# A four-layer network in one kernel: the skip term of the second scan summed by TensorE, and another order of the first mixer chunk

## The chip, the cores and the metric

The kernel runs on one core of a Trainium2 chip. Its time is the device time of one execution in microseconds (us); the median over several executions is compared. The engines run side by side and wait for each other through semaphores: TensorE (PE), VectorE (DVE), ScalarE (ACT), GpSimd (POOL), and the queue of SyncE (SP), from which all DMAs are issued.

## What is computed

2048 tokens of 128 numbers pass four layers, each added to its input. Cut to what matters here:

```python
x = L0_attn_u                                                  # 1 x 2048 x 128
x = x + _L0_attn_ref(_layernorm(x), ...)   # "mixer": projection, causal conv, state-space scan of 8 heads, gate
x = x + _L0_ffn_ref(_layernorm(x), ...)    # causal attention of 16 heads, then 8 experts, 2 per token
x = x + _L1_attn_ref(_layernorm(x), ...)   # "scan": the layer below
x = x + _L1_ffn_ref(_layernorm(x), ...)    # "net": a gated net of 512 hidden values

# of the mixer, for each token t and head:
h = exp(dt_t * A) * h + dt_t * x_t * B_t ;  y_t = C_t . h + D * x_t
# of the scan layer, for each of 256 channels and 16 states:
h = exp(-delta * n) * h + delta * B_n * u
y = h.sum(-1)
y = y + u * D          # the skip term, D is one number per channel
y = y * silu(z)
return y @ out_proj_w + out_proj_b
```

## The kernel before

All is written by hand: each engine has its own list of instructions, and `wait_ge` and `then_inc` on named semaphores order them. Work goes in 4 blocks of 512 tokens (`NB`, `BLK`), and the mixer's recurrence in 16 chunks of 128 tokens (`g` = 0 to 15, four to a block, `TPB`). The layers stand one behind the other: mixer, attention, experts, scan, net; the first parts of a layer are drawn into the end of the one ahead of it.

**The mixer.** A block's front has five parts: (0) norm of the rows and their transpose `x0T`; (1) and (2) projections into five PSUM banks used in a ring, and the first conv taps on VectorE; (3) the running sum `cs` of `dt*A` (four scans, `cs_done`), the last conv taps, the convolved projections of x (`L475`), the SiLUs `xs` on ScalarE, and on GpSimd `bdec` and `cdec` (`L749`, `L750`, `dec_done`); and the gated skip (`L736`), whose place is VectorE's part 2. Block 0's front runs by itself at the start, and block b+1's is spread over the chunks of block b. `cs` also goes to DRAM and comes back spread over the partitions as `cs_bc`, by SP.

A chunk g has a front on TensorE, `chunk_front_pe`: transposes of dt, cs and bdec into bank `turn_a` (`L488` to `L490`), of x into `turn_b` (`L494`, `L495`), and a small product there (`L496`). The semaphore `turned` counts two for each chunk. VectorE's `chunk_front_dve` copies them out (`dt_tok`, `ncs_tok`, `bd_tok`, `xdt`, counted by `tok_dve`), ScalarE makes `edec` (`L638`, 8 exponentials), GpSimd makes it causal in two halves (`L647`), VectorE multiplies it with the product (`mdec`, `L775`, `m_done`), and `chunk_back_pe` of the chunk ahead follows on TensorE (`L508` to `L515`), whose sums VectorE takes up (`L785` to `L794`). TensorE's list has the front of chunk g ahead of the back of chunk g-1.

Block 1's norm belongs to part 0 of its front, so on VectorE it stands ahead of `mdec` of chunk 0, and on GpSimd its root (`L394`, in `ln_pool`) behind the two causal masks of chunk 0:

```python
if part == 0 and b <= 1:
    ...
    ln_stats_dve(o, dve, b, src)        # waits for GpSimd's root
    ln_apply_dve(dve, b, src, xn, 0)
```

**The scan.** For each block and each of the 16 states, GpSimd makes `drive` (5 slots), ScalarE `decay` (2 slots), VectorE runs two scans into `hst` (4 slots, `L2164`), and TensorE adds `hst` to two PSUM banks with the identity as weights (`state_sum_pe`, `L2083`), three states later. After the third state of the next block VectorE takes the sums up (`scan_y_dve`):

```python
for j in range(2):
    n = o.did(dve.scalar_tensor_tensor(bank[j], u[:, j, :], C("d1", j), bank[j], ALU.mult, ALU.add))
dve.wait_ge(S["sz_ready"], b + 1)
for j in range(2):
    o.wait(n - 1 + j)
    ins = dve.tensor_tensor(u[:, j, :], bank[j], sz1[b % 2][:, j, :], ALU.mult)
ins.then_inc(S["y1_ready"], 1)
```

TensorE's sums of the next block and ScalarE's part "z" of the block after it wait for `y1_ready`. The last block's turn stands behind all scans, beside the net's first products.

Of the kernel before, what the change touches and what calls it, by code (L numbers as in the profile page):

```python
# [5 lines left out]
F32 = mybir.dt.float32  # L6
# [6 lines left out]
P = 128  # L13
# [83 lines left out]
def build(nc, a):  # L97
# [24 lines left out]
    with ctx:  # L122
# [104 lines left out]
        qk_r = sb("qk_r", [P, 2, BLK], F32)  # L227
        assert BASE + free[0] <= nc.sbuf_usable_end
# [102 lines left out]
        assert free[0] <= W_END, (free[0], W_END)  # L331
        free[0] = t_end["sz1_even"]
# [148 lines left out]
        def chunk_front_pe(pe, g):  # L481

            b, c = divmod(g, TPB)
            cc = slice(c * P, (c + 1) * P)
            pe.wait_ge(S["dec_done"], b + 1)
            if g >= 1:
                pe.wait_ge(S["tok_dve"], 4 * g - 1)
            pe.transpose(turn_a[:, 0:P], dt[b % 2][:, cc], ident[:, :])  # L488
            pe.transpose(turn_a[:, P:2 * P], cs[b % 2][:, cc], ident[:, :])
            pe.transpose(turn_a[:, 2 * P:3 * P], bdec[b % 2][:, cc], ident[:, :]).then_inc(S["turned"], 1)  # L490
            if g >= 1:
                pe.wait_ge(S["m_done"], 2 * g)
# [201 lines left out]

        def front_early_dve(o, dve, b, part):

            if part == 0 and b <= 1:
                if b == 1:
                    dve.wait_ge(S["in_rest"], 16)
                src = x_tok[:, b * TPB:(b + 1) * TPB, :]  # L700
                ln_stats_dve(o, dve, b, src)
                ln_apply_dve(dve, b, src, xn, 0)
            elif part == 2:
# [35 lines left out]
        def front_pool(o, pool, b, part):  # L739
            if part == 0:  # L740
                if b <= 1:
                    ln_pool(pool, b)
            elif part == 3:
# [13 lines left out]
        def chunk_front_dve(dve, g):  # L757
# [1046 lines left out]
        def moe_act(o, act):  # L1804
            for k in range(N_UNITS + 2):
# [91 lines left out]
        SUM_AFTER = 3  # L1897
        NET_STATS, NET_LN, NET_APPLY, NET_TURN, NET_HI = 7, 9, (11, 12), 13, 14
# [179 lines left out]
        def state_sum_pe(pe, b, n):  # L2078
# [5 lines left out]
            ins.then_inc(S["summed"], 1)  # L2084

# [87 lines left out]
        def scan_y_dve(o, dve, b):  # L2173
# [301 lines left out]
        def _(pool):  # L2475
# [16 lines left out]
            front_pool(o, pool, 0, 0)  # L2492
# [45 lines left out]
        def _(act):  # L2538
# [25 lines left out]
        def _(dve):  # L2564
# [170 lines left out]
```

## Time and profile before

| | us |
|---|---|
| median of 3 runs | 1248.2 (1247.94 to 1252.96) |
| the profiled execution | 1252.22 |
| its span in the profile | 1249.9 |
| PE busy | 1120.0 (90% of the span) |
| DVE busy | 931.8 (75%) |
| ACT busy | 783.9 (63%) |
| POOL busy | 327.6 (26%) |

The profiled execution has 2.3 us around its span and is 4 us over the median. The shares are means over layers that have little in common: the mixer takes the first 200 us or so, attention and experts the stretch up to 910 us, the scan that from 910 to 1111 us, the net the rest. GpSimd, with 26% of the whole, works through nearly all of the scan. The granted TensorE clock is 0.969 in the mean.

### The profile page before, as it was taken

To read this page: it belongs to the slowest core of one execution; us is meant where nothing else is said; L and a number is where in the kernel's file an instruction comes from. 1 tells how busy PE (TensorE), PEld (TensorE's weight loads), DVE (VectorE), ACT (ScalarE), POOL (GpSimd) and SP (SyncE) were. 2 spreads that over 40 slices of the span, in tenths; PEclk is the share of its full clock that TensorE was granted. 3 is DMA by queue.
4 is the path that set the end of the run, shared out by engine and by line. 5 is a ranking of instruction groups with operands and counts; after the bars stand their busy time and mean duration, and the time that the engine had idled before them with its cause. 6 is when DMAs were issued, how large, how long until landed. Compare 5 with 4: busy or idle time off the path is not lost.

```text
span 1249.9 us, 16003 instructions
## 1 busy us (share of the span) xinstructions
PE 1120.0 (90%) x5702; PEld 594.1 (48%) x5702; DVE 931.8 (75%) x1737; ACT 783.9 (63%) x1156; POOL 327.6 (26%) x271
## 2 busy tenths in 40 slices
PE   5889878888999999989999899999979789799998
PEld 2455554443333333333322288887633334357776
DVE  4788678857887888878864188887789999984432
ACT  4767632455655656656678898667758677455554
POOL 4233332210000000000012131210179788840000
PEclk9789889999998999999999999999989999899999
DMA  5211464345000000000000132211223222200000
GB/s 152 79 41 69 122 148 102 86 102 119 2 1 1 2 1 2 1 1 1 2 19 12 42 109 66 78 51 36 84 84 111 85 110 93 102 1 6 4 9 18
DMA packets 30623, 67.29 MB, mean 54 GB/s; under 512 B 3952, under 2 KB 16240, under 8 KB 28496
## 3 DMA queue, kind: packets, MB, share of 16 engines
q1 hardware_dynamic: 30544, 66.27, 18.5%
q8 instruction: 46, 0.75, 0.3%
q14 instruction: 33, 0.27, 0.1%
HBM read 57.47 MB, written 8.78 MB: 53 GB/s over the span
## 4 chain that ended last, share of the span: by engine, by line
PE 57%; DVE 14%; POOL 9%; issue 8%; ACT 7%; DMA 1%; SPq 0%; DVEq 0%; POOLq 0%; ACTq 0%
PE psum L1353 8%; PE psum L1238 8%; PE psum L405 7%; PE psum L407 7%; PE psum L406 7%; PE psum L1307 7%; POOL drive L2142 6%; DVE mx L1250 6%; DVE hst L2164 2%; ACT probs L1321 2%; PE psum L551 1%; PE psum L543 1%; PE psum L475 1%; PE psum L1956 1%; DMA m_rows<-mrow 1%
## 5 line engine op out<-in xcount | busy, mean ns | idle before, releaser
L1250 DVE TENSOR_REDUCE mx<-psum 128x1 f32<-128x512 f32 (+3 forms) x640 | 349.2, 603 | 64.8 <-PE psum L1238 35.2
L1321 ACT ACTIVATE probs<-psum 128x1024 f32<-128x1024 f32 (+1 forms) x320 | 283.6, 936 | 173.7 <-PE psum L1307 152.7
L1238 PE MATMUL psum<-kz,qa 128*128 128x512 bf16 (+3 forms) x640 | 199.3, 354 | 18.5 <-DVE mx L1250 12.8
L1307 PE MATMUL psum<-qa,kz 128*128 128x512 bf16 (+1 forms) x640 | 176.2, 363 | 7.8 <-DMA qa<-m_rows 4.4
L2142 POOL TENSOR_TENSOR drive<-du,b_bc 128x1024 f32<-128x1024 f32 x64 | 149.5, 2367 | 10.6 <-DVE hx_lo L675 9.1
L1353 PE MATMUL psum<-probs,v 128*32 128x512 f32 (+3 forms) x1280 | 150.8, 541 | 1.5 <-POOL probs L1332 1.4
L1238 PEld LDWEIGHTS psum<-kz,qa 128*128 128x128 bf16 x640 | 57.2, 97 | 180.5 <-DVE mx L1250 131.9
L2083 PE MATMUL psum<-hst,ident 128*128 128x512 f32 x256 | 120.3, 614 | 22.7 <-DVE u L2182 14.1
L1332 POOL TENSOR_SCALAR_AFFINE_SELECT probs<-probs 128x512 f32<-128x512 f32 x48 | 29.4, 637 | 361.1 <-ACT probs L1321 361.1
L2164 DVE TENSOR_TENSOR_SCAN hst<-psum,hlast,drive 128x512 f32<-128x512 f32 x96 | 115.2, 1261 | 8.7 <-ACT psum L2096 5.0
L675 DVE TENSOR_TENSOR hx_lo<-hid,hx_hi 128x1024 fp32r<-128x1024 f32 x64 | 81.4, 1276 | 33.9 <-ACT hx_hi L1679 29.8
L2096 ACT ACTIVATE psum<-delta 128x1024 f32<-128x1024 f32 x64 | 65.6, 1026 | 51.5 <-DVE hst L2164 51.4
L1673 ACT ACTIVATE hid<-psum,cols 128x512 f32<-128x512 f32 x128 | 81.5, 681 | 21.2 <-PE psum L407 21.0
L2083 PEld LDWEIGHTS psum<-hst,ident 128*128 128x128 f32 x256 | 48.4, 196 | 88.7 <-issue 68.1
L1307 PEld LDWEIGHTS psum<-qa,kz 128*128 128x128 bf16 x640 | 57.6, 99 | 68.1 <-ACT probs L1321 27.3
L675 DVE TENSOR_TENSOR fh_lo<-fh,fh_hi 128x512 fp32r<-128x512 f32 x48 | 32.1, 688 | 57.7 <-ACT fh_hi L2371 57.7
L405 PE MATMUL psum<-fh_hi,fw_lo 128*128 128x512 f32 x144 | 57.9, 402 | 3.6 <-DVE fh_lo L675 3.6
L407 PE MATMUL psum<-fh_hi,fw_hi 128*128 128x512 f32 x144 | 56.9, 395 | 0.0
L406 PE MATMUL psum<-fh_lo,fw_hi 128*128 128x512 f32 x144 | 56.7, 394 | 0.0
L1241 PE MATMUL psum<-identb,maskneg 128*128 128x128 bf16 x256 | 55.5, 221 | 0.0
L405 PE MATMUL psum<-nx_hi,ew_lo 128*128 128x512 f32 x128 | 52.5, 411 | 3.2 <-ACT hid L1673 2.2
L2370 ACT ACTIVATE fh<-psum,cols 128x512 f32<-128x512 f32 x32 | 22.1, 689 | 48.9 <-PE psum L407 48.9
(294 smaller groups left out, 1944.6 us busy)
## 6 DMA issues: line engine op xcount, KB each, us to landing
b_bc<-b_rows SPq DMA_DIRECT2D x16, 1024.0 KB, 4.7
cs_bc<-cs_rows SPq DMA_DIRECT2D x16, 512.0 KB, 4.8
gate_bc<-gate_rows SPq DMA_DIRECT2D x32, 256.0 KB, 3.1
qk_part_rows<-qk_parts SPq DMA_DIRECT2D x48, 128.0 KB, 2.3
ew_raw<-experts_dram SPq DMA_DIRECT2D x8, 512.0 KB, 3.6
qa<-qk_part_rows SPq DMA_DIRECT2D x16, 192.0 KB, 5.3
kz<-qk_part_rows SPq DMA_DIRECT2D x16, 192.0 KB, 5.8
fw_raw<-net_dram SPq DMA_DIRECT2D x11, 256.0 KB, 2.7
```

Source lines behind the costliest of these rows:

```text
L405: pe.matmul(out, w[1], x[0], start=start, stop=False, skip_group_check=True)
L406: pe.matmul(out, w[0], x[1], start=False, stop=False, skip_group_check=True)
L407: return pe.matmul(out, w[0], x[0], start=False, stop=stop, skip_group_check=True)
L675: return dve.tensor_tensor(out, value, hi.bitcast(F32), ALU.subtract)
L1238: ins = pe.matmul(out[:, 0:w], qa[:, b, h // 2, i * P:(i + 1) * P], key_rows(h, c)[:, 0:w], start=True, stop=not last, skip_group_check=True)
L1250: dve.tensor_reduce(mx[:, 4 * i + h % 4, c:c + 1], fill_bank("mx", k, n)[:, 0:w], AX.X, ALU.max).then_inc(S["mx_read"], 1)
L1307: ins = pe.matmul(out[:, lo:], key_rows(h, kt // TPB)[:, kt % TPB * P:(kt % TPB + 1) * P], qa[:, b, h // 2, lo:], start=True, stop=not dia ...
L1321: act.activation(probs[:, st % 2, hh, :, lo:], s_pair[n % 2][:, :, lo:], ACT.Exp, scale=SCALE).then_inc(S["p_done"], 1)
L1353: ins = pe.matmul(out[32 * hh:32 * hh + 32, own:], v9[:, at:at + 32], probs[:, st % 2, hh, j, own:], start=(kt == 0), stop=(kt == TPB * (b ...
L2083: ins = pe.matmul(bank[j][:, :], ident[:, :], hst[:, (NS1 * b + n) % HBUF, j, :], start=(n == 0), stop=(n == NS1 - 1))
L2142: pool.tensor_tensor(drive[:, k % DRIVE_SLOTS, :, :], du[:, b % 2, :, :], rows.unsqueeze(1).broadcast_to([P, 2, BLK]), ALU.mult).then_inc( ...
L2164: ins = dve.tensor_tensor_scan(hst[:, k % HBUF, j, :], decay[k % 2][:, j, :], drive[:, k % DRIVE_SLOTS, j, :], init, ALU.mult, ALU.add)
```

## The change

1. `scan_y_dve` loses its two `scalar_tensor_tensor`. In their place ScalarE makes once, in the experts' part, two diagonal matrices of D (`d_diag`), and `state_sum_pe` adds two products of `d_diag` with `u1` to the same banks, behind the sum of state 2 of each block.
2. In block 0's front, VectorE's running sum and the last conv taps stand ahead of the gated skip; block 1's statistics stand ahead of block 0's first conv taps, and its application (`xn`) between `ncs_tok` and `bd_tok` of chunk 0. GpSimd makes block 1's root right behind block 0's.
3. The transpose of bdec moves from `turn_a` to the end of `turn_b`. The front of a chunk waits for `cs_done` in place of `dec_done`, which only the moved transpose waits for; `bd_tok` is copied behind the second count of `turned`.
4. ScalarE has one exponential of one column (`table_ahead`) ahead of chunk 0, and SP issues the two saves of `blank` (1 MB) ahead of chunk 8's load in place of chunk 3's.

```diff
         def chunk_front_pe(pe, g):
-            pe.wait_ge(S["dec_done"], b + 1)
+            pe.wait_ge(S["cs_done"], b + 1)
             if g >= 1:
-                pe.wait_ge(S["tok_dve"], 4 * g - 1)
+                pe.wait_ge(S["tok_dve"], 4 * g - 2)
             pe.transpose(turn_a[:, 0:P], dt[b % 2][:, cc], ident[:, :])
-            pe.transpose(turn_a[:, P:2 * P], cs[b % 2][:, cc], ident[:, :])
-            pe.transpose(turn_a[:, 2 * P:3 * P], bdec[b % 2][:, cc], ident[:, :]).then_inc(S["turned"], 1)
+            pe.transpose(turn_a[:, P:2 * P], cs[b % 2][:, cc], ident[:, :]).then_inc(S["turned"], 1)
             if g >= 1:
+                pe.wait_ge(S["tok_dve"], 4 * g)
                 pe.wait_ge(S["m_done"], 2 * g)
             pe.wait_ge(S["xs_ready"], 4 * b + 4)
...
-            pe.matmul(turn_b[:, 2 * P:3 * P], ...).then_inc(S["turned"], 1)
+            pe.matmul(turn_b[:, 2 * P:3 * P], ...)
+            pe.wait_ge(S["dec_done"], b + 1)
+            pe.transpose(turn_b[:, 3 * P:4 * P], bdec[b % 2][:, cc], ident[:, :]).then_inc(S["turned"], 1)
...
         def mixer_sp(sp):
-                if g == CS_SLOTS:
+                if g == 2 * TPB:
                     blank_save_sp(sp)
...
+        def first_norm_dve(o, dve, b):
+            if b == 1:
+                dve.wait_ge(S["in_rest"], 16)
+            src = x_tok[:, b * TPB:(b + 1) * TPB, :]
+            ln_stats_dve(o, dve, b, src, wait=(b == 0))
+            if b == 0:
+                ln_apply_dve(dve, b, src, xn, 0)
...
         def chunk_front_dve(dve, g):
-            dve.tensor_copy(bd_tok[:, s, :], turn_a[:, 2 * P:3 * P]).then_inc(S["tok_dve"], 1)
+            if g == 0:
+                dve.wait_ge(S["ln_rstd"], 2)
+                ln_apply_dve(dve, 1, x_tok[:, TPB:2 * TPB, :], xn, 0)
             dve.wait_ge(S["turned"], 2 * g + 2)
+            dve.tensor_copy(bd_tok[:, s, :], turn_b[:, 3 * P:4 * P]).then_inc(S["tok_dve"], 1)
...
         def state_sum_pe(pe, b, n):
             ins.then_inc(S["summed"], 1)
+            if n == SKIP_AFTER:
+                pe.wait_ge(S["c_u_read"], 2 * b + 2)
+                for j in range(2):
+                    pe.matmul(bank[j][:, :], d_diag[:, j, :], u1[:, b % 2, j, :], start=False, stop=False)
...
         def scan_y_dve(o, dve, b):
-            for j in range(2):
-                n = o.did(dve.scalar_tensor_tensor(bank[j][:, :], u[:, j, :], C("d1", j), bank[j][:, :], ALU.mult, ALU.add))
             dve.wait_ge(S["sz_ready"], b + 1)
             for j in range(2):
-                o.wait(n - 1 + j)
                 ins = dve.tensor_tensor(u[:, j, :], bank[j][:, :], sz1[b % 2][:, j, :], ALU.mult)
...
         # moe_act
+                if k == Y_MOVE:
+                    for j in range(2):
+                        act.activation(d_diag[:, j, :], ident[:, :], ACT.Identity, scale=C("d1", j))
...
         # GpSimd's list
-            front_pool(o, pool, 0, 0)
+            ln_pool(pool, 0)
+            ln_pool(pool, 1)
...
         # ScalarE's list
             for n in range(5):
                 front_act(o, act, 0, n)
+            act.activation(table_ahead[:, :], one[:, 0:1], ACT.Exp)
...
         # VectorE's list
-            for n in range(5):
+            first_norm_dve(o, dve, 0)
+            front_late_dve(o, dve, 0, 0)
+            first_norm_dve(o, dve, 1)
+            for n in range(1, 4):
                 front_early_dve(o, dve, 0, n)
-                front_late_dve(o, dve, 0, n)
+            front_late_dve(o, dve, 0, 2)
```

VectorE from the first norm to `mdec` of chunk 0, before (`L371` to `L387` are a norm, `L686` and `L689` conv taps, `L717` the running sum, `L736` the gated skip, `L775` mdec):

```order
L387 TENSOR_SCALAR xn<-x_tok,ln_mv,ln_rs 128x128 x4
L726 MEMSET convin 128x2x3
L686 TENSOR_SCALAR cacc<-convin,cols 128x512 x2
L689 SCALAR_TENSOR_TENSOR cacc<-convin,cols,cacc 128x512 x2
L736 TENSOR_TENSOR skip<-psum,sz 128x512 x2
L711 TENSOR_SCALAR dtA<-dt_even,a_neg 128x512
L717 SCALAR_TENSOR_TENSOR cs_even<-one,dtA 128x128 x4
L689 SCALAR_TENSOR_TENSOR cacc<-convin,cols,cacc 128x512 x4
...
L764 COPY bd_tok<-psum 128x128
L767 TENSOR_TENSOR xdt<-psum,dt_tok 128x256
L371 BN_STATS ln_st<-x_tok 128x6 x4
...
L387 TENSOR_SCALAR xn<-x_tok,ln_mv,ln_rs 128x128 x4
L775 TENSOR_TENSOR mdec<-edec,psum 128x512 x2
```

The same stretch after (line numbers of the changed kernel: `L718` and `L724` the running sum, `L743` the gated skip, `L782` mdec):

```order
L374 BN_STATS ln_st<-x_tok 128x6 x4
L377 BN_AGGR ln_mv<-ln_st 128x2 x4
L382 TENSOR_SCALAR ln_ve<-ln_mv 128x4
L691 TENSOR_SCALAR cacc<-convin,cols 128x512 x2
L694 SCALAR_TENSOR_TENSOR cacc<-convin,cols,cacc 128x512 x2
L718 TENSOR_SCALAR dtA<-dt_even,a_neg 128x512
L724 SCALAR_TENSOR_TENSOR cs_even<-one,dtA 128x128 x4
L694 SCALAR_TENSOR_TENSOR cacc<-convin,cols,cacc 128x512 x4
L743 TENSOR_TENSOR skip<-psum,sz 128x512 x2
...
L390 TENSOR_SCALAR xn<-x_tok,ln_mv,ln_rs 128x128 x4
L772 COPY bd_tok<-psum 128x128
L774 TENSOR_TENSOR xdt<-psum,dt_tok 128x256
L782 TENSOR_TENSOR mdec<-edec,psum 128x512 x2
```

The skip went behind the running sum, the second norm's statistics ahead of the conv taps, and its application ahead of `bd_tok`, so that nothing of it stands between `xdt` and `mdec` any more.

TensorE at a chunk's front, before:

```order
L488 MATMUL psum<-ident,dt_even 128x128
L489 MATMUL psum<-ident,cs_even 128x128
L490 MATMUL psum<-ident,bdec_even 128x128
L494 MATMUL psum<-ident,xs_even 128x128
L495 MATMUL psum<-ident,xs_even 128x128
L496 MATMUL psum<-xs_even 128x128
```

and after:

```order
L491 MATMUL psum<-ident,dt_even 128x128
L492 MATMUL psum<-ident,cs_even 128x128
L497 MATMUL psum<-ident,xs_even 128x128
L498 MATMUL psum<-ident,xs_even 128x128
L499 MATMUL psum<-xs_even 128x128
L501 MATMUL psum<-ident,bdec_even 128x128
```

There are as many instructions; the one that needs GpSimd's product stands last.

## Rows read from the trace of the kernel before

**Rows 1.** Timeline, first 41 us: start, us, work, idle ahead and releaser.

```profile
2.29 0.43 SPq L2456 DMA_DIRECT2D x_tok<-x_dram  x1
...
12.52 3.23 POOL L2497 TENSOR_TENSOR wk<-w_raw,tap_bc 128x256 f32<-128x256 f32 x4 [5.46 <-DMA tap_bc<-taps_dram]
...
13.10 0.49 DVE L686 TENSOR_SCALAR cacc<-convin,cols 128x512 f32<-128x512 f32 x1 [4.87 <-ACT convin L581]
...
18.36 7.03 PE L475 MATMUL psum<-x0T,wk 128*128 128x512 f32 x16
...
18.66 1.29 DVE L736 TENSOR_TENSOR skip<-psum,sz 128x512 f32<-128x512 f32 x2 [1.70 <-ACT sz L590]
...
20.37 2.03 DVE L717 TENSOR_TENSOR_SCAN cs_even<-one,dtA 128x128 f32<-128x128 f32 x4
...
24.34 1.28 SPq L620 DMA_DIRECT2D cs_bc<-cs_rows  x3
...
26.79 1.24 ACT L606 ACTIVATE xs_even<-psum,cols 128x512 f32<-128x512 f32 x2
...
29.50 0.47 PE L488 MATMUL psum<-ident,dt_even 128*128 128x128 f32 x1 [4.11 <-POOL cdec_even L750]
...
30.75 1.28 ACT L638 ACT_TABLE_LOAD   x1 [2.73 <-DVE ncs_tok L763]
...
32.05 2.44 ACT L638 ACTIVATE edec<-cs_bc,ncs_tok 128x128 f32<-128x128 f32 x8
...
34.56 0.64 POOL L647 TENSOR_SCALAR_AFFINE_SELECT edec<-edec 128x512 f32<-128x512 f32 x1 [0.53 <-ACT edec L638]
...
35.16 1.01 POOL L394 TENSOR_TENSOR ln_rs<-ln_ve,mhalf 128x4 f32<-128x4 f32 x1
36.21 1.12 DVE L387 TENSOR_SCALAR xn<-x_tok,ln_mv,ln_rs 128x128 f32<-128x128 f32 x4 [2.81 <-POOL ln_rs L394]
37.24 1.28 DVE L775 TENSOR_TENSOR mdec<-edec,psum 128x512 f32<-128x512 f32 x2
...
39.00 0.42 PE L494 MATMUL psum<-ident,xs_even 128*128 128x128 f32 x1
...
40.28 1.08 PE L508 MATMUL psum<-mdec,xdt 128*32 128x128 f32 x16
```

**Rows 2.** DMA issues, first 40 us: size of one, median us to landing.

```profile
cs_bc<-cs_rows SPq DMA_DIRECT2D x4, 512.0 KB, 5.1
...
x_tok<-x_dram SPq DMA_DIRECT2D x1, 768.0 KB, 8.7
```

**Rows 3.** Timeline of PE and DVE where block 1 begins.

```profile
65.45 0.44 PE L488 MATMUL psum<-ident,dt_odd 128*128 128x128 f32 x1 [3.06 <-POOL cdec_odd L750]
...
67.39 1.08 PE L508 MATMUL psum<-mdec,xdt 128*32 128x128 f32 x16
...
74.12 0.42 DVE L767 TENSOR_TENSOR xdt<-psum,dt_tok 128x256 f32<-128x256 f32 x1 [0.32 <-PE psum L496]
```

**Rows 4.** Busy time by engine in two stretches of the scan.

```profile
960.00:1010.00 50.00, 42.03 (x111) 18.43 (x110) 47.40 (x54) 35.88 (x60) 41.89 (x24) 1.00 0.28 101
1010.00:1060.00 50.00, 42.83 (x108) 18.79 (x107) 45.93 (x45) 35.19 (x60) 43.56 (x22) 0.97 0.29 101
```

**Rows 5.** Timeline where block 1 of the scan is taken up.

```profile
1022.12 1.39 DVE L2178 SCALAR_TENSOR_TENSOR psum<-u,cols,psum 128x512 f32<-128x512 f32 x2
1023.42 1.28 DVE L2182 TENSOR_TENSOR u<-psum,sz_odd 128x512 f32<-128x512 f32 x2
...
1024.85 10.43 PE L2083 MATMUL psum<-hst,ident 128*128 128x512 f32 x20 [3.24 <-DVE u L2182]
...
1028.61 2.46 DVE L2164 TENSOR_TENSOR_SCAN hst<-psum,hlast,drive 128x512 f32<-128x512 f32 x2 [1.55 <-PE psum L2083]
```

**Rows 6.** Timeline of PE, one block earlier.

```profile
974.81 8.82 PE L2083 MATMUL psum<-hst,ident 128*128 128x512 f32 x20 [3.24 <-DVE u L2182]
```

**Rows 7.** Timeline, the net's first products.

```profile
1114.54 0.19 PEld L405 LDWEIGHTS psum<-xT_hi,fw_lo 128*128 128x128 f32 x1 [0.35 <-DVE u L2182]
```

More of the change, by code:

```diff
@@ L227, in build @@
         qk_r = sb("qk_r", [P, 2, BLK], F32)
+        table_ahead = sb("table_ahead", [P, 1], F32)
         assert BASE + free[0] <= nc.sbuf_usable_end
@@ L331, in build @@
         assert free[0] <= W_END, (free[0], W_END)
+        d_diag = sb("d_diag", [P, 2, P], F32)
+        assert t_end["ew_hi3"] <= t_end["fo"] <= t_end["d_diag"] - 1024 and t_end["d_diag"] <= A_END
         free[0] = t_end["sz1_even"]
@@ L495, in chunk_front_pe @@
             pe.transpose(turn_b[:, P:2 * P], xs[b % 2][:, 1, cc], ident[:, :])
-            pe.matmul(turn_b[:, 2 * P:3 * P], xs[b % 2][0:NS0, 2, cc], xs[b % 2][0:NS0, 3, cc], start=True, stop=True).then_inc(S["turned"], 1)
+            pe.matmul(turn_b[:, 2 * P:3 * P], xs[b % 2][0:NS0, 2, cc], xs[b % 2][0:NS0, 3, cc], start=True, stop=True)
+            pe.wait_ge(S["dec_done"], b + 1)
+            pe.transpose(turn_b[:, 3 * P:4 * P], bdec[b % 2][:, cc], ident[:, :]).then_inc(S["turned"], 1)
         def chunk_back_pe(pe, g):
@@ L693, in conv0_dve @@
                         ins.then_inc(S["conv_done"], 1)
-        def front_early_dve(o, dve, b, part):
[L697 to L703, printed above, removed]
+        def first_norm_dve(o, dve, b):
[5 more added lines that the diff above has]
+                ln_apply_dve(dve, b, src, xn, 0)
+        def front_early_dve(o, dve, b, part):
+            if part == 2:
                 dve.wait_ge(S["conv_hist"], b + 1)
@@ L739, in front_pool @@
         def front_pool(o, pool, b, part):
[L740 to L743, printed above, removed]
+            if part == 3:
                 if b >= 2:
@@ L1897, in build @@
         SUM_AFTER = 3
+        SKIP_AFTER = 2
         NET_STATS, NET_LN, NET_APPLY, NET_TURN, NET_HI = 7, 9, (11, 12), 13, 14
```

## The prediction

> **What bounds the kernel now.** I read the page's engine rows first, then the timelines of the stretches that the change touches: the first chunk, the first block boundary of the mixer, the scan, and the join of scan and net. TensorE is busy for 90% of the whole (the table of the page's rows above), so what the change does to VectorE counts only where VectorE, or a chain through it, decides. There are two such places.
>
> The first is chunk 0 [rows 1]. VectorE waits 1.70 us for ScalarE's SiLU before it may do the gated skip (1.29 us), and only then runs the sum that ends at 22.40. TensorE has nothing after the convolved projections end at 25.39 and waits 4.11 us for GpSimd's `cdec`. The exponentials run from 32.05 to 34.49 and the second causal mask ends at 35.20. mdec could start then, but GpSimd makes block 1's root behind the masks (to 36.17), VectorE waits 2.81 us for it, applies the norm (1.12 us), and mdec runs from 37.24 to 38.52. TensorE's next transposes of x start at 39.00.
>
> The second is the scan. In two stretches of 50 us VectorE is busy for 47.40 and 45.93 us, TensorE for 42.03 and 42.83, GpSimd for 41.89 and 43.56 [rows 4]: VectorE is the fullest. At a block's turn [rows 5] its two `scalar_tensor_tensor` start at 1022.12, and the products with the gate follow at 1023.42 and end at 1024.70. TensorE has waited 3.24 us for them and begins the next sums at 1024.85. So what VectorE loses there, TensorE and ScalarE lose too.
>
> **Chunk 0, worked out.** Without wait and skip ahead of it the running sum ends 1.70 + 1.29 = 3.0 us earlier, at 19.4. TensorE's projections do not move and still end at 25.39 [rows 1]: they are the new bound. From there: the last SiLU of x, half of the 1.24 us of two, 0.64 with its hand-over, to 26.05; ScalarE's table load, 1.28, to 27.35; the one-column exponential, 0.2 by my estimate, to 27.5; the eight of edec, 2.44, to 29.95; the last mask, 0.64 with a hand-over of 0.07, to 30.7; the second half of mdec, 0.64, to 31.4. Before it was 38.52: 7.1 us earlier.
>
> What has to be in time for that: `cs_bc`. Its loads were issued at 24.34, 1.94 after the sum ended, so they go out at 21.4, and with 5.1 us to landing [rows 2] the first lands by 26.5, one ahead of 27.5. The rest of x is issued at 2.29 and takes 8.7 to land, at 11.0; block 1's statistics then stand ahead of conv taps that start at 13.10, after 4.87 us of waiting for ScalarE [rows 1], and cost about 1.4, so they lie in a wait of VectorE. On GpSimd the root (1.0) would end near 13.5 and push the four products `wk` (3.23 us from 12.52) to end at about 16.8, before TensorE wants them at 18.36. The application of block 1's norm (1.12) stands behind `ncs_tok`, while ScalarE loads its table, and is done by 28.5 even where GpSimd's `cdec` holds it up. Both edits I cost at nothing; if the rest of x came 2 us later, the taps would be late by as much, with 3 us of slack behind them.
>
> Then TensorE. It went on at 39.00, and goes on at 31.45, since the transposes of dt and cs are already done: 7.55 us. One more transpose (bdec) now stands between it and the products with mdec, 0.2 us at the pace of this stretch, where one takes 0.21 from start to start (0.42 with its overlap). **7.3 us** arrive at the products that began at 40.28. From there on every wait of the mixer is for another engine or for a DMA issued by one; nothing waits for a fixed time. I let the whole shift pass.
>
> **The other chunks.** At block 1's begin TensorE waits 3.06 us for `cdec` and begins three plus three transposes and products at 65.45; the back of chunk 3 starts at 67.39 [rows 3]. Afterwards only the bdec transpose is left at that moment: the back starts at about 65.9, **1.5 us** earlier. ScalarE bounds it from above: its exponentials of chunk 4 wait for VectorE, which is busy until the old moment, so I take no more; the bound from below is nothing. At blocks 2 and 3 TensorE has other work when GpSimd ends, and nothing is won. Against this stands the copy `bd_tok`, which filled VectorE's wait for `turned`: at chunk 5 VectorE waited 0.32 for the small product ahead of `xdt` [rows 3]. Now the copy of 0.28 comes behind it, and the transpose too. I take 0.3 at each of chunks 5, 9 and 13, where such a wait is on the path, and 0.1 at chunk 15: **1.0 us lost**. The mixer: 7.3 + 1.5 - 1.0 = **7.8 us**.
>
> The save of blank goes out while the first load for chunk 8 would; 1 MB at the rates of such transfers is some 3 us, and `cs_bc` is not wanted until after a table load. Nothing, with 2 us as its other bound.
>
> **The scan.** Three turns lie within it and each loses 1.39 us of VectorE [rows 5], for which TensorE, ScalarE and, through ScalarE's split of weights, GpSimd were waiting: 3 x 1.39 = **4.2 us**. The fourth lies beside the net's first products; TensorE waited only 0.35 us for it [rows 7]: **0.35**. The two added products cost TensorE what the sum of one state does. Five sums took 8.82 us at full clock [rows 6], 1.76 each, so 7 us over four blocks. They come after the sum of state 2. TensorE has 7 to 8 us free of every 50 [rows 4], and behind the added pair the next that needs it is VectorE's state 7, whose hst slot is that of state 3. After the turn TensorE takes 3 sums, the pair and one more: 5 x 1.76 = 8.8 us. VectorE takes state 3, waits, and has states 4 to 6 to do, at 2.46 each 9.8 us and more with the conv taps. It fits by 1 us. I cost the pair at nothing. The two diagonals on ScalarE are under 1 us once, beside TensorE's experts: nothing, at most 0.8. The scan: **4.5 us**.
>
> **Sum.** 7.8 + 4.5 = 12.3 us. The profiled execution took 1252.22, 1249.9 of it the span, and would take 1239.9. It is 4.0 over the median of the runs shown, so against 1248.2 the forecast is 1235.9, 1.0% less. Less than 0.5%, 6.2 us, is about what a measurement of this kernel cannot tell from no change.
>
> The page "ScalarE: Activation LUTs" of the Trainium skill, under "What ACT_TABLE_LOAD costs", gives a switch of table about 2.66 us with its drain. The row has 1.28 and the first exponential starts 0.02 behind it; by the page's figure the new chain of chunk 0 would be 1.4 longer and the forecast 1237.3. I keep the row's.
>
> **Rivals.**
>
> *Only the scan's part arrives.* The mixer from chunk 1 on might be held by something that chunk 0 does not move: TensorE's projections of block 1, or VectorE, that is nearly full there. For it: the stretch holds many short waits with changing releasers. Against it: all of them hang from chunk 0 by `xdt`, `mdec` or the norm. If 5 of the 7.8 are lost: 1248.2 - 2.8 - 4.5 = 1240.9. Chance 0.15.
>
> *GpSimd takes over the scan.* It has 41.89 and 43.56 busy of 50 [rows 4]; without the 1.4 us each block still has about 48.6 us for it. That leaves 5 us, but it stands in order behind ScalarE's splits and the norm. Should each turn give back all: 1248.2 - 7.8 - 0.35 = 1240.0. Chance 0.1.
>
> *The clock helps.* After a wait of 3.24 us TensorE did its 20 instructions once in 8.82 us and once in 10.43 [rows 5, 6], the latter begun at 1.2 GHz in place of 2.4, and VectorE then waited 1.55 us. Shorter waits may keep 2.4 GHz: 1.6 us at one or two turns and some 2 us at chunks 1 and 4: down to 1248.2 - 12.3 - 4 = 1232. Chance 0.12.
>
> *Slower: the burst at a turn runs at the low clock to its end.* The added pair makes it longer. At 1.2 GHz three sums, the pair and a sum are 5 x 3.5 = 17.6 us, VectorE would wait for state 7's slot some 7 us at each of three turns, 21 us, and the time would be 1248.2 - 12.3 + 21 = 1257. It decides once a burst stays low for over about 14 us; the longest low stretch at a turn cost only 10.43 - 8.82 = 1.6 us in all. Chance 0.04.
> The Trainium skill ("TensorE: Matmul & The Clock Gate", "Part 1: The HAM clock gate") says that activity releases the throttle; by that rule a dense burst cannot stay low, and the trace agrees, since 20 instructions lost 1.6 us and not 8.8.
>
> *The forecast*, within 3 us of 1235.9: 0.59.
>
> **Range and chances.** The likeliest case gives 1236. The range reaches down to the clock's case and up over the two in which one part is lost, with 1 to 3 us for the spread of runs: 1230.5 to 1244. Faster by over 0.5% means below 1242.0: the forecast and the clock's case whole, nearly all of GpSimd's, over half of the first rival: 0.84. Within 0.5%: 0.12. Slower: 0.04.
>
> **What would show it.** In the profile after: mdec of chunk 0 ends near 31.4, and TensorE's wait ahead of chunk 0's transposes is gone; no `ln_rs` behind the masks of chunk 0; the back of chunk 3 starts some 9 us earlier than 67.39; the attention begins about 8 us earlier. In the scan VectorE's turn has two instructions, 1.28 us, and the turns stand 1.4 us closer together; VectorE does not wait for a sum ahead of state 7. Wrong would be: a wait of `wk` or of the conv taps that reaches TensorE before 25.4, `cs_bc` landing behind 27.5, new waits of VectorE behind TensorE in the scan, or a mixer that ends less than 5 us earlier.

## The result, and the profile after

| | median (lowest to highest), us | executions |
|---|---|---|
| before | 1247.93 (1244.80 to 1252.98) | 20 |
| after | 1244.38 (1238.15 to 1248.34) | 20 |

The ratio is 0.9965, 95% interval [0.9951, 0.9979]: 0.35% less, where 1.0% was forecast. One kernel's executions spread over 8 to 10 us here, more than the effect, and the two profiled executions don't stand alike in their spreads: that of before (1252.22) among the longest, that of after (1239.12) among the shortest. So the profiles differ by 12.8 us of span (1249.9 to 1237.1), which is near the 12.3 forecast by the luck of these two executions alone; the medians differ by 3.6. Three runs of the changed kernel together (37 executions) have a mean of 1243.5, and the kernel before (all 129 executions) 1248.6: 5.1 ± 1.0 us. (Means ± are two standard errors throughout; a kernel is compared with the kernel before by these means.)

Chunk 0 of the changed kernel, from the timeline (start, us, work, idle ahead and releaser), against [rows 1]:

```profile
12.37 2.97 POOL L2511 TENSOR_TENSOR wk<-w_raw,tap_bc 128x256 f32<-128x256 f32 x4
13.18 0.88 DVE L691 TENSOR_SCALAR cacc<-convin,cols 128x512 f32<-128x512 f32 x1 [1.88 <-ACT convin L586]
14.76 3.73 DVE L691 TENSOR_SCALAR cacc<-convin,cols 128x512 f32<-128x512 f32 x1 [0.69 <-ACT convin L586]
15.28 2.04 POOL L2512 MEMSET v<- 128x2336 f32 x1
17.26 0.95 POOL L2513 MEMSET blank<- 128x1024 bf16 x1
...
18.96 7.03 PE L478 MATMUL psum<-x0T,wk 128*128 128x512 f32 x16
...
21.29 1.66 DVE L724 TENSOR_TENSOR_SCAN cs_even<-one,dtA 128x128 f32<-128x128 f32 x4
...
27.34 1.24 ACT L611 ACTIVATE xs_even<-psum,cols 128x512 f32<-128x512 f32 x2
...
28.60 1.28 ACT L2559 ACT_TABLE_LOAD   x1
...
30.00 2.43 ACT L643 ACTIVATE edec<-cs_bc,ncs_tok 128x128 f32<-128x128 f32 x8
...
33.17 0.69 DVE L782 TENSOR_TENSOR mdec<-edec,psum 128x512 f32<-128x512 f32 x1 [0.48 <-POOL edec L652]
...
35.68 1.08 PE L513 MATMUL psum<-mdec,xdt 128*32 128x128 f32 x16
```

The order is the new one: no root of block 1 behind the masks, the table load under way before the exponentials are wanted, mdec ended at 33.86 in place of 38.52, the products with it begun at 35.68 in place of 40.28. But the running sum ends at 22.95, not at 19.4: the second conv tap, a `tensor_scalar` of 512 columns, takes 3.73 us, from 14.76 to 18.49, while GpSimd ends the fourth `wk` and fills v and blank (to 18.21). In the profile of the kernel before the same tap took 0.49 at 14.68, and the fills began behind its end:

```profile
14.68 0.49 DVE L686 TENSOR_SCALAR cacc<-convin,cols 128x512 f32<-128x512 f32 x1 [1.09 <-ACT convin L581]
15.69 2.04 POOL L2498 MEMSET v<- 128x2336 f32 x1
```

Behind the late sum everything that ScalarE does is late: the last SiLU ends at 28.58, where 26.05 was forecast.

TensorE where block 1 begins, against [rows 3]: first the turns of chunk 4 and the back of chunk 3 (`L513`), then the turns of chunk 5:

```profile
59.74 0.30 PE L497 MATMUL psum<-ident,xs_odd 128*128 128x128 f32 x1 [1.20 <-DVE mdec L782]
...
60.84 0.33 PE L501 MATMUL psum<-ident,bdec_odd 128*128 128x128 f32 x1 [0.28 <-POOL cdec_odd L754]
61.10 0.65 PE L513 MATMUL psum<-mdec,xdt 128*32 128x128 f32 x16
...
64.89 0.27 PE L492 MATMUL psum<-ident,cs_odd 128*128 128x128 f32 x1
67.12 0.44 PE L497 MATMUL psum<-ident,xs_odd 128*128 128x128 f32 x1 [1.96 <-issue]
```

The back of chunk 3 starts 6.3 us earlier than 67.39, where some 9 were forecast.

And the scan: busy time in two stretches (us; PE, PEld, DVE, ACT, POOL; granted clock, DMA share, GB/s), against [rows 4]:

```profile
950.00:1000.00 50.00, 45.07 (x117) 19.87 (x116) 47.40 (x54) 36.80 (x62) 43.22 (x24) 1.00 0.29 101
1000.00:1050.00 50.00, 44.71 (x116) 19.49 (x114) 46.37 (x46) 35.67 (x60) 44.63 (x23) 1.00 0.29 103
```

Its timeline at a turn, against [rows 5], and at the last one, against [rows 7]:

```profile
1011.81 1.26 DVE L2195 TENSOR_TENSOR u<-psum,sz_odd 128x512 f32<-128x512 f32 x2
1012.99 2.45 DVE L2180 TENSOR_TENSOR_SCAN hst<-psum,hlast,drive 128x512 f32<-128x512 f32 x2
1013.22 5.39 PE L2094 MATMUL psum<-hst,ident 128*128 128x512 f32 x12 [1.92 <-DVE u L2195]
1016.54 2.46 DVE L2180 TENSOR_TENSOR_SCAN hst<-psum,hlast,drive 128x512 f32<-128x512 f32 x2 [1.10 <-ACT psum L2112]
1018.44 1.88 PE L2100 MATMUL psum<-u,d_diag 128*128 128x512 f32 x4
...
1098.75 0.79 PE L408 MATMUL psum<-xT_hi,fw_lo 128*128 128x512 f32 x1
1099.35 1.29 DVE L2195 TENSOR_TENSOR u<-psum,sz_odd 128x512 f32<-128x512 f32 x2 [1.50 <-PE psum L2094]
```

TensorE's wait at the turn is 1.92 for 3.24. The turns end at 964.35, 1013.07 and 1061.79: 48.72 apart, where they were 50.04 and 50.48 apart. At the last turn VectorE waits 1.50 us for the sums, as it did before, with the net's first product already begun. The same two rows of the kernel before:

```profile
1111.28 0.79 PE L405 MATMUL psum<-xT_hi,fw_lo 128*128 128x512 f32 x1
1111.88 1.42 DVE L2178 SCALAR_TENSOR_TENSOR psum<-u,cols,psum 128x512 f32<-128x512 f32 x2 [1.50 <-PE psum L2083]
```

### The profile page after: what moved, and what is told of

It reads as the page before. It is cut to its first block, busy times and chain, and to the rows that moved or that the text cites. A ratio compares the mean times of both kernels' runs of the same rounds, so it can differ in the third digit from the quotient of the medians.

```text
span 1237.1 us, 16014 instructions
## 1 busy us (share of the span) xinstructions
PE 1121.7 (91%) x5718; PEld 593.2 (48%) x5718; DVE 931.8 (75%) x1729; ACT 783.7 (63%) x1159; POOL 327.7 (26%) x271
## 4 chain that ended last, share of the span: by engine, by line
PE 58%; DVE 13%; POOL 9%; issue 8%; ACT 7%; DMA 1%; SPq 0%; DVEq 0%; POOLq 0%; ACTq 0%
PE psum L1360 8%; PE psum L1245 8%; PE psum L408 8%; PE psum L410 7%; PE psum L409 7%; PE psum L1314 7%; POOL drive L2158 6%; DVE mx L1257 6%; ACT probs L1328 2%; DVE hst L2180 1%; PE psum L556 1%; PE psum L548 1%; PE psum L478 1%; PE psum L2094 1%; PE psum L1967 1%
```

## The experiments

All were timed in five rounds beside the kernel before.

| run | edit | median (range), us | of before | ratio [95%] | mean granted clock |
|---|---|---|---|---|---|
| e1 | before, unchanged | 1248.09 (1245.9 to 1252.4) | 1247.84 | 0.9993 [0.9979, 1.0008] | 0.972 |
| e2 | after, unchanged | 1242.30 (1239.0 to 1244.9) | 1247.84 | 0.9941 [0.9920, 0.9961] | 0.975 |
| e3 | before + scan's part | 1243.20 (1236.6 to 1248.8) | 1247.84 | 0.9958 [0.9938, 0.9977] | 0.974 |
| e4 | after without scan's part | 1246.54 (1241.7 to 1251.4) | 1247.84 | 0.9980 [0.9960, 0.9999] | 0.972 |
| e5 | before + turns' part | 1248.93 (1245.1 to 1254.5) | 1248.30 | 0.9997 [0.9975, 1.0019] | 0.970 |
| e6 | e4 without turns' part | 1246.15 (1241.7 to 1248.2) | 1248.30 | 0.9984 [0.9964, 1.0003] | 0.971 |
| e7 | e4, GpSimd's fills later | 1248.41 (1244.8 to 1251.6) | 1248.30 | 0.9996 [0.9978, 1.0015] | 0.968 |
| e8 | after, GpSimd's fills later | 1242.04 (1240.3 to 1246.8) | 1248.30 | 0.9954 [0.9936, 0.9971] | 0.972 |
| e9 | before + idle-time matmuls | 1245.08 (1243.3 to 1249.9) | 1247.23 | 0.9990 [0.9971, 1.0009] | 0.978 |
| e10 | after + idle-time matmuls | 1238.48 (1236.4 to 1240.9) | 1247.23 | 0.9933 [0.9914, 0.9952] | 0.980 |
| e11 | e8 + idle-time matmuls | 1237.05 (1233.3 to 1239.9) | 1247.23 | 0.9920 [0.9899, 0.9941] | 0.981 |
| e12 | after without turns' part | 1238.68 (1235.6 to 1242.8) | 1247.23 | 0.9938 [0.9915, 0.9961] | 0.976 |
| e13 | after, unchanged | 1242.79 (1239.3 to 1246.8) | 1247.76 | 0.9958 [0.9938, 0.9979] | 0.974 |
| e14 | e12 once more | 1238.87 (1235.8 to 1242.0) | 1247.76 | 0.9912 [0.9887, 0.9937] | 0.977 |
| e15 | e12, GpSimd's fills later | 1239.95 (1235.6 to 1241.4) | 1247.76 | 0.9916 [0.9892, 0.9939] | 0.976 |
| e16 | e15 + idle-time matmuls | 1234.83 (1233.1 to 1236.6) | 1247.76 | 0.9884 [0.9864, 0.9904] | 0.981 |

Where some of them stand in their profiled executions (ends in us; mdec of a chunk, `drive` 0 with which the scan begins):

| run | cs | mdec 0 | mdec 3 | mdec 4 | mdec 11 | drive 0 | end | end - drive 0 |
|---|---|---|---|---|---|---|---|---|
| before | 22.40 | 38.52 | 64.24 | 73.18 | 135.02 | 909.92 | 1249.87 | 339.95 |
| e1 | 22.59 | 38.66 | 64.01 | 71.39 | 133.02 | 908.08 | 1248.78 | 340.70 |
| after | 22.95 | 33.86 | 59.63 | 67.03 | 130.92 | 901.04 | 1237.10 | 336.06 |
| e2 | 22.66 | 33.56 | 59.33 | 66.72 | 129.35 | 902.78 | 1239.62 | 336.84 |
| e3 | 22.65 | 38.64 | 64.00 | 71.38 | 133.02 | 908.39 | 1244.63 | 336.24 |
| e4 | 22.68 | 33.58 | 59.36 | 66.74 | 130.63 | 899.69 | 1240.83 | 341.14 |
| e5 | 22.78 | 36.34 | 62.43 | 69.82 | 134.06 | 903.86 | 1244.95 | 341.09 |
| e7 | 18.86 | 30.97 | 56.87 | 64.25 | 128.28 | 905.92 | 1247.64 | 341.72 |
| e14 | 22.89 | 35.13 | 60.12 | 67.52 | 129.15 | 901.40 | 1237.85 | 336.45 |
| e16 | 18.58 | 32.93 | 55.99 | 63.39 | 125.66 | 897.60 | 1234.04 | 336.44 |

**Both kernels again, and each half alone** (e1 to e4). e3's edit to the kernel before:

```diff
+ for j in range(2): pe.matmul(bank[j][:, :], d_diag[:, j, :], u1[:, b % 2, j, :], start=False, stop=False)
- for j in range(2): n = o.did(dve.scalar_tensor_tensor(bank[j][:, :], u[:, j, :], C("d1", j), bank[j][:, :], ALU.mult, ALU.add))
```

and e4 is the changed kernel with the reverse of it. Expected:

> The kernel before, unchanged, profiled a second time. Theory A (parts add up, and which times TensorE's clock falls decides several us from run to run): ratio 1.00; the profile may differ from the first by 1 to 5 us, and where it does, the shift arises in stretches where the granted clock differs. Theory B (before has one fixed time): the same span within 1 us at every checkpoint.

> The changed kernel, unchanged, profiled a second time. Theory A: 0.9965 again within its interval (about 4 us faster), and the profile shows the mixer 4 to 7 us and the scan 4 to 5 us earlier whatever the total is; if the total is less than their sum, the loss is in stretches where the clock is lower. Theory C (the first chunk gained only 5 us, and the rest of the mixer gives some back): the shift at the end of the mixer is under 4 us.

> Only the skip term is moved to TensorE; the mixer is that of before. Theory A: 4.5 us faster than before (ratio 0.9964), turns 1.4 us closer together. Rival (GpSimd takes over, or TensorE's burst is held up): 1 us or less.

> The mixer's part of the change alone; the scan is that of before (the scan's skip term on VectorE again). Theory A: mdec of chunk 0 ends 4.7 us earlier as in the changed kernel, and 5 to 6 us arrive (ratio 0.995 to 0.996). Theory C: what chunk 0 gains is given back by the copy of bdec and by later waits, and the ratio is 0.999 or more.

From `drive` 0 to the end the three profiles with the scan's part (after, e2, e3) take 336.4 us in the mean, before, e1 and e4 340.6: 4.2 less. Alone it is worth 5.1 ± 2.1 us in the means. The mixer's half (e4) is 5.1 us ahead of e1 at mdec 0, 2.4 at mdec 11, and worth 2.6 ± 1.9. So the missing part is the mixer's. e1 also shows that 1.6 of the 8.9 us between mdec 3 and mdec 4 in the profile of before belong to its clock, which was at the low level there: in e1 the stretch is 7.38, and in the changed kernel 7.40.

**The turns' part alone, and the front without it** (e5, e6). e5's edit to the kernel before:

```diff
-            pe.wait_ge(S["dec_done"], b + 1)
+            pe.wait_ge(S["cs_done"], b + 1)
-            pe.transpose(turn_a[:, 2 * P:3 * P], bdec[b % 2][:, cc], ident[:, :]).then_inc(S["turned"], 1)
+            pe.wait_ge(S["dec_done"], b + 1)
+            pe.transpose(turn_b[:, 3 * P:4 * P], bdec[b % 2][:, cc], ident[:, :]).then_inc(S["turned"], 1)
```

> The kernel before, with the turns alone changed: the transpose of bdec last, the front waiting for the running sum, its copy behind the second count. Theory A (each piece keeps what it wins up to the scan): mdec of chunk 0 ends 2 to 3 us earlier, since ScalarE's exponentials no longer wait for GpSimd; later chunks lose 0.5 us where the copy comes late; ratio 0.998. Theory C (the turns give back in the later chunks what they win in the first): ratio 1.000 or more, and the loss shows at chunks 5, 9 and 13.

> The mixer's part without the turns: running sum ahead of the gated skip, block 1's norm moved, the exponential ahead, the save of blank moved; transposes as before. Theory A: mdec of chunk 0 ends about 4 us earlier (no root and no norm between the masks and mdec), and the later chunks lose nothing, ratio 0.997. Theory C: the ratio is as that of the whole mixer part or better, 0.998 or less, and the loss at chunk 9 is gone.

Alone it wins 2.3 us at mdec 0 and has lost it by chunk 8; at mdec 11 it is 1.0 behind e1. TensorE's waits at the same place, first in e5 and then in e14, where the turns are as before:

```profile
69.92 0.30 PE L494 MATMUL psum<-ident,xs_odd 128*128 128x128 f32 x1 [1.95 <-issue]
```

```profile
61.33 0.33 PE L491 MATMUL psum<-ident,dt_odd 128*128 128x128 f32 x1 [2.69 <-POOL cdec_odd L752]
...
67.57 0.33 PE L497 MATMUL psum<-ident,xs_odd 128*128 128x128 f32 x1 [0.96 <-DVE mdec L780]
```

A wait of 2.69 ahead of chunk 4 is gone with the turns' part (it is 1.20 and 0.29 there), and one of 0.96 at chunk 5 has become 1.95. In the timed means e5 is 0.4 ± 1.9 over before, and e4 0.4 ± 2.3 over e6: nothing to be seen yet.

**The held tap** (e7, e8). GpSimd's fills move behind its masks of chunks 1 and 2:

```diff
-            pool.memset(v9[:, :], 1.0).then_inc(S["v_ones"], 1)
-            o.did(pool.memset(blank[:, :, :], 1.0))
...
+                if g == 1:
+                    pool.memset(v9[:, :], 1.0).then_inc(S["v_ones"], 1)
+                if g == 2:
+                    o.did(pool.memset(blank[:, :, :], 1.0))
```

> The mixer's part alone, and GpSimd's fills of v and blank go behind the masks of chunks 1 and 2, off block 0's front. Theory P (GpSimd's fills held VectorE's second conv tap for 3.3 us, so the running sum did not come earlier): the tap takes 0.5 to 1 us instead of 3.7, the running sum ends near 19.5 to 20.5 instead of 22.7, and mdec of chunk 0 ends 1.5 to 2.2 us earlier than 33.6. Rival (TensorE's projections or the SiLUs bound it anyway): the sum moves, but mdec of chunk 0 stays within 0.5 us of 33.6.

> The whole changed kernel with the same move of GpSimd's fills. Theory P: 1.5 to 2.2 us less than the changed kernel, ratio to the kernel before 0.993 to 0.995. Rival: no less than the changed kernel, 0.9955 to 0.9965.

The timeline of e7:

```profile
12.70 3.14 POOL L2506 TENSOR_TENSOR wk<-w_raw,tap_bc 128x256 f32<-128x256 f32 x4
...
14.43 0.84 DVE L691 TENSOR_SCALAR cacc<-convin,cols 128x512 f32<-128x512 f32 x1 [0.71 <-ACT convin L586]
...
25.71 1.28 ACT L2556 ACT_TABLE_LOAD   x1
```

With nothing of GpSimd behind `wk` the tap takes 0.84, the sum ends at 18.86, and mdec 0 at 30.97, where the prediction had 31.4: 7.55 under before. In e8 mdec 0 ends at 32.00, 6.5 under. The working for chunk 0 was right but for this one hold. The Trainium skill ("SBUF — State Buffer", "Who interferes with whom") says that VectorE and GpSimd share a pair of ports, that a `tensor_scalar` can want both pairs, and that who issues first keeps it for its whole instruction. The trace agrees, and shows something more: the tap was ready in the middle of the fourth `wk`, and two further instructions of GpSimd went ahead of it. But the time did not follow: e7 is 2.1 ± 2.3 slower than e4, e8 0.7 ± 1.6 faster than after. In e7's profile the lead of 4.7 us over e1 at mdec 11 is 2.2 at `drive` 0, and in the stretch from 65 to 135 us its granted clock was 0.91, where e1's was 1.00. This led to the theory called C from here on: what the mixer wins is taken back by TensorE's clock, which falls to 1.2 GHz after waits, and the change puts these waits elsewhere. (Rival F: the clock's low stretches have nothing to do with these waits.)

**TensorE kept busy in its waits** (e9 to e11). Matmuls whose result nobody reads, 0.06 us each, at four waits of the mixer in e9 (221 matmuls) and at five in e10 and e11 (136). Nothing is left out of the computation.

```diff
+        def busy_pe(pe, n, done):
+            if done:
+                pe.wait_ge(S["y_done"], done)
+            for _ in range(n):
+                pe.matmul(ys_bank[:, 0:P], identb[:, :], maskneg[:, :], start=True, stop=True)
```

> The kernel before with TensorE kept busy in four of its waits in the mixer: matmuls of 128 columns whose result nobody reads (60 ahead of chunk 0's turns, 85 ahead of block 1's norm turns, 42 ahead of chunk 4's turns, 34 ahead of the first norm turns for attention; some 4 to 5 us each at full clock). Nothing of the computation changes. Theory C (the time of a run is set by how much of the mixer and of attention's beginning runs at TensorE's lower clock, and the waits of TensorE there bring the clock down): the granted clock stays at 1 through the mixer after its first rise, the mean clock of the runs rises from .971 to above .975, the spread of the runs shrinks, and the median falls by 2 to 4 us, ratio 0.997 to 0.998. Rival F (the clock's stretches have nothing to do with these waits): mean clock .971, ratio 1.000 to 1.002, the last from the fillers that delay real work.

> The changed kernel with fillers of the same kind in the waits that it has in the same part (34 behind chunk 0's first two turns, 28 behind chunk 1's, 14 behind chunk 4's, 26 behind chunk 5's, 34 ahead of the first norm turns for attention). Against the kernel before with fillers: theory C says the mixer's lead of 4.1 us by chunk 11 now reaches the end with the scan's 4.2, so 8.3 us, 7 to 9.5. Rival F: the lead goes where it went, and the difference is the 5.1 us that the changed kernel has over all its runs so far, 4 to 6. Chunk 11's masked decays end near 130.9 us either way, and drive 0 begins 7 to 9 us ahead of that kernel's by theory C.

> The changed kernel with the fillers of the run before and with GpSimd's fills of v and blank behind the masks of chunks 1 and 2, so that VectorE's second tap isn't held and chunk 0 is done 7 us earlier than before. Theory C: against the kernel before with fillers 6.5 us in the mixer and 4.2 in the scan, 10.7 us, 9 to 12, the fastest of all kernels so far, near 1234 to 1237. Rival F: 5.9 us as it had without fillers.

Against e9, e10 is 7.9 ± 2.2 us faster and e11 9.6 ± 2.5 (8.3 and 10.7 by theory C, 5.1 and 5.9 by F); by the medians 6.6 and 8.0, between the two. The matmuls take 2.3 ± 1.6 off the kernel before, 5.1 ± 1.8 off the changed one and 6.1 ± 2.4 off e8. So the change is worth 2.8 ± 2.4 us more with them, and e8 3.8 ± 2.9. This surplus does not show theory C, since the kernels don't carry the same matmuls: e9 has 85 ahead of block 1's norm turns, where e10 and e11 have none. Within a kernel a run's time falls by 0.68 us for each 0.001 of mean granted clock (266 executions of fourteen kernels). By that, e9 is 2.4 ± 0.8 us slower than its clock would have it, e10 and e11 are not (-0.1 ± 0.9 and 0.1 ± 1.5). A cost of e9's own matmuls is a rival that accounts for most of the surplus, and no run tests it. Busy time and granted clock by stretch, first of before and then of e9 (the clock is the third number from the right):

```profile
24.00:65.00 41.00, 28.36 (x132) 16.21 (x130) 27.14 (x77) 28.14 (x59) 11.96 (x14) 0.79 0.36 116
65.00:135.00 70.00, 64.05 (x355) 37.91 (x356) 59.88 (x168) 52.10 (x113) 19.90 (x23) 0.95 0.15 53
135.00:184.00 49.00, 38.00 (x214) 24.27 (x213) 30.70 (x99) 21.67 (x50) 18.45 (x19) 0.83 0.66 153
```

```profile
24.00:65.00 41.00, 36.93 (x346) 25.49 (x345) 28.73 (x84) 29.55 (x62) 12.64 (x14) 1.00 0.34 117
65.00:135.00 70.00, 62.74 (x366) 36.41 (x364) 60.91 (x167) 52.67 (x115) 21.61 (x24) 1.00 0.17 62
135.00:184.00 49.00, 40.60 (x255) 26.82 (x256) 34.13 (x105) 24.77 (x55) 20.35 (x21) 0.90 0.67 156
```

**The turns' part left out, once more, and the same with the other two edits** (e12 to e16). e16 has the matmuls at the waits that remain there.

> The change without the part on the turns: the running sum put ahead, the norm of block 1 in a later wait and the scan's skip term by TensorE, while each chunk's three turns stay as they were before. By its parts alone (3.1 us for the first, 5.2 for the scan in the mean of the runs so far): 1240 us, 8 us under before, ratio 0.9935, and about 3 us under the changed kernel. If the turns' part costs nothing and the 0.5 us by which the front alone did better was chance, it is the changed kernel's time, ratio 0.996.

> The changed kernel once more, beside the version of the next run. It has had 1243.7 us in the mean of 26 executions and 1242.3 in the last call: median 1241.5 to 1244.5, ratio 0.994 to 0.9965.

> The change without its part on the turns, once more. Theory T (the turns' part costs: 0.5 us at chunk 9 and up to 1.9 at chunk 5, with the clock): 2 to 4 us under the changed kernel of the same call, 1238 to 1240.5. Rival L (the six executions of the last call fell well; the turns' part changes nothing in the mean): within 1 us of it.

> The version of the run before with GpSimd's fills of v and blank behind the masks of chunks 1 and 2, so that VectorE's second tap isn't held. Chunk 0's masked decays end near 31.8 instead of 34.9. Theory K (the clock takes back what the mixer wins, since the waits come to stand elsewhere): as in the two pairs so far, mean within 1 us of the run before, 1237.5 to 1240.5. If the 3 us arrive: 1235 to 1237.

> The same with matmuls of 128 columns that nobody reads in four of TensorE's waits in the mixer (40 ahead of chunk 0's turns, 18 ahead of chunk 1's values, 42 ahead of chunk 4's turns, 34 ahead of the first norm turns for attention). Theory K: clock at 1 through the mixer, mean clock .980 or above, 1233 to 1236, 3 to 5 us under the same kernel without them and the fastest of all. Rival: no more than 1 us under it, the fillers' gain in the changed kernel having been chance.

On one chip, in one set of runs, e14 is 3.9 us below e13 by the medians, and the pooled means (e12 and e14, 12 executions, against the changed kernel's 37) are 4.7 ± 1.7 apart: theory T over L. e15 is level with it (0.0 ± 2.5) though its mdec 11 stands 2.5 to 4.9 us earlier, and e16 is 3.9 ± 2.3 below e15, as theory K said. That is not clear of the 2.3 ± 1.6 that the matmuls take off the kernel before, so it shows that they pay, and not that the clock had taken the 2.5 to 4.9 us. The stretches of e15, then of e16:

```profile
24.00:65.00 41.00, 33.83 (x179) 20.05 (x178) 29.20 (x80) 30.69 (x69) 18.40 (x21) 0.88 0.23 77
65.00:135.00 70.00, 62.04 (x344) 35.22 (x344) 59.70 (x167) 52.57 (x110) 21.95 (x23) 0.98 0.23 74
135.00:184.00 49.00, 40.62 (x228) 26.30 (x228) 31.93 (x97) 22.21 (x53) 19.25 (x20) 0.85 0.71 158
```

```profile
24.00:65.00 41.00, 36.68 (x298) 23.82 (x297) 30.49 (x85) 32.03 (x74) 18.41 (x21) 1.00 0.25 89
65.00:135.00 70.00, 65.25 (x367) 38.18 (x367) 59.51 (x167) 52.33 (x109) 22.32 (x24) 0.98 0.20 69
135.00:184.00 49.00, 40.47 (x233) 25.87 (x232) 34.13 (x102) 22.41 (x50) 18.89 (x20) 0.90 0.74 172
```

e16 is the fastest, 1.2% under before. Without matmuls that do nothing the fastest are the kernel of e12 and e14 and that of e15, level with each other. All of them beat the changed kernel.

## Why the prediction was wrong

The direction was right, the size was not: 12.3 us forecast, 3.6 to 5.5 measured by the medians of three sets of runs, 5.1 ± 1.0 by the means. The scan's term held; the mixer's, 7.8 us, did not: its half alone (e4) is worth 2.6 ± 1.9. Seven of the eight combinations of the three parts were run (the kernel before is one); fitted as a sum of parts they give 3.3 ± 1.2 us for the front, 2.0 ± 1.1 lost for the turns, 4.4 ± 1.1 for the scan. The parts don't add up strictly (the turns cost nothing visible without the scan's part and 4.7 with it; why is open).

1. *"The scan: 4.5 us"* held. The turns are 1.3 and 1.8 us closer together, `drive` 0 to the end is 4.2 shorter. The net's first product parts these 4.2 us: from `drive` 0 to it, where the three turns lie, after, e2 and e3 take 198.1 us in the mean and before, e1 and e4 202.0, 4.0 less for 4.2 forecast; from it to the end they take 138.3 to 138.4 where the others take 138.5 to 138.6, about 0.25 for 0.35 forecast. The added pair costs nothing seen: VectorE's wait behind the turn is 1.10, for ScalarE. The rival of GpSimd as the new bound and that of a burst at the low clock are refuted: GpSimd is at 43.22 and 44.63 of 50, and the clock was 1.00 in both stretches.

2. *"7.3 us arrive at the products that began at 40.28"* was the mis-sized term: it measured 4.6 there (35.68), 4.7 at mdec 0, and 5.0 in e2 against before. The step that failed is "Without wait and skip ahead of it the running sum ends 3.0 us earlier, at 19.4": it ended at 22.95, later than the 22.40 of before. I took the taps at the duration that the kernel before happened to show (0.49). e7 gives 7.55 at mdec 0 and e8 6.5, for 7.1 forecast, so the rest of the chain was sized rightly. That hold was not new: e1, the same kernel as before, has it too, at 2.94 us, and there it only takes the place of VectorE's wait for ScalarE's SiLU:

```profile
14.64 2.94 DVE L686 TENSOR_SCALAR cacc<-convin,cols 128x512 f32<-128x512 f32 x1 [0.80 <-ACT convin L581]
...
19.52 1.27 DVE L736 TENSOR_TENSOR skip<-psum,sz 128x512 f32<-128x512 f32 x2
```

What I took for a row's duration was one outcome of two, and the rarer one: of the thirteen profiles with the fills in their old place, twelve hold the first or the second tap. But the hold is not the whole of the missing time: with it gone e8 is only 0.7 ± 1.6 us faster than the changed kernel.

3. *"1.5 us earlier"* at block 1's begin was not there to win. At full clock the stretch from mdec 3 to mdec 4 is 7.4 us with and without the change; the row that I read it from, TensorE's wait of 3.06, ended at the start of a stretch of low clock, and what decides is ScalarE's exponentials behind VectorE, which I had named as the bound from above. The turns' loss, forecast as 1.0, is 0.3 to 1.6 at chunk 5 (mdec 4 to mdec 5, against e1) and 0.5 at chunk 9. Behind chunk 0, where they give about 1 us (mdec 0 ends at 34.86 in e6), they were forecast to win 0.5; over the whole kernel they lose 2.0 ± 1.1.

4. *"I let the whole shift pass."* It does not pass. Against e1, whose clock was full there, the lead of 5.0 us at mdec 0 is 2.1 to 3.7 at mdec 11 in the three profiles of the changed kernel: the turns take 0.5 at chunk 9 and 0.3 at chunk 5, there 1.4 to 1.6 where the clock is low behind the new wait (after, e13; not e2). The 4.1 that the profiled pair shows at mdec 11 hold 2.0 us of low clock of the kernel before. From mdec 11 to the 20th of attention's 640 maxima (`mx`, on VectorE) the profiles without matmuls in the waits take from 64.7 us (e6, e12, e14, clock 0.95) to 71.9 (e8, 0.83): 7.2 us apart, more than what the mixer wins ahead of it, and the longer at the lower clock. From a lead of 4.7 at mdec 11 e7 keeps 0.5 ± 1.5 in the mean, while e12 and e14, 1.5 and 3.9 ahead there, end 9.8 ahead with the scan's 4.2 in it. The rival "only the scan's part arrives" (1240.9) came nearest, but not by its mechanism, TensorE's projections or VectorE. That the clock takes back part of the mixer's gain is argued, not shown. For it stands that e7's mean clock is 0.0046 ± 0.0028 under e4's, some 3.1 us by the 0.68 above, as an estimate; the matmuls in the waits leave it open. The rival by which the clock helps got its sign right and no more: the mean clock rose from 0.9714 to 0.9730, which is 1.1 us.

5. *"It is 4.0 over the median of the runs shown"* I had as an offset to be subtracted. It was a sign that this profile holds several us of low clock which another execution of the same kernel does not, and that single rows from it, such as those of points 2 and 3, may be one outcome of several. The range should have taken in the 8 us that one kernel spreads over.

What stays open: why the turns' part costs 4.7 us beside the scan's part and nothing visible without it. Of these, 2.6 us go with the mean clock (0.9730 for 0.9768, at 0.68 us for each 0.001). Where they arise the profiles show in part: by mdec 11 e14 and e2 differ by 0.2 us, at the 20th maximum by 5.8. The stretch between, first in e14 and then in e2:

```profile
129.15:193.85 64.70, 51.59 (x303) 31.53 (x302) 44.46 (x137) 29.41 (x63) 24.65 (x24) 0.95 0.58 141
```

```profile
129.35:199.63 70.28, 56.77 (x301) 34.62 (x302) 44.79 (x137) 29.39 (x63) 24.48 (x24) 0.88 0.56 130
```

The work is the same, TensorE is 5.2 us longer busy with it, and the clock is 0.88 for 0.95. The three profiles with the front's part, without the turns' and with the fills in place (e6, e12, e14) have 64.7 here, the four with the turns' part too (after, e2, e4, e13) 65.5 to 70.3. Attention gives 2.8 of the 5.8 back (433.9 us in e2, 436.7 in e14). Which wait lets the clock fall there is not shown.

## What to carry to other kernels

A shift early in this kernel did not simply pass to its end, and the stretches in which it was lost or won were those of a lower or higher clock: ask which waits of TensorE a shift moves, and look at two profiles of the kernel before, not one, ahead of reading a wait or a duration off it. A VectorE instruction that stands beside GpSimd's work can have two durations (0.5 to 1.0 us and 2.9 to 3.9 here); where it becomes critical by the change, cost it by the longer one and ask what GpSimd issues next. And try the parts of a change one by one: here the version with one part less was faster than the whole.

## What the runs showed of the hardware

A `tensor_scalar` of 128x512 f32 (a conv tap of block 0) took 0.49 to 0.99 us free and 2.9 to 3.9 us beside GpSimd. The long form came in twelve of the thirteen profiles with the two memsets (2.04 and 0.95) right behind `wk`: in ten at the second tap, in e3 and e9 at the first. In all twelve the first memset began between 0.3 ahead of the tap's start and 0.7 behind it, and the tap ended some 0.3 us behind the second memset. In the profile of before, where the memset began 1.0 behind the tap's start and after its end, and in the five with the memsets moved, no tap was held.

The same code of attention (the stretch from the 20th to the 639th maximum) took 433.6 to 438.2 us in the eighteen profiles, by where the low-clock stretches fell. The Trainium skill ("TensorE: Matmul & The Clock Gate", "Part 1: The HAM clock gate") says that the gate runs free of the kernel's start, so that one kernel meets it differently from run to run. The runs are in line with it: the kernel before has a mean clock of 0.964 to 0.979 and 1241.8 to 1253.5 us from one execution to the next, and here that is larger than the change's effect.
